# A transformer layer on one core: one GpSimd power moved ahead of a weight piece, the last high part given to VectorE, the final sums copied by token tile

## What is computed

```
h = patches @ W + b                        # 768 -> 192
q, k, v = split(h @ w_qkv.T)               # 12 heads of 64; q and k scaled by a norm over the heads
out = softmax(q k^T / scale) v             # 36 tokens of one image
h1 = layernorm(h + out @ w_out.T + b_out)                         # "LN1"
logits = h1 @ Wr + br                      # 8 experts, the two best are taken, softmax of the two
gate, up = split(min(h1 @ Wgu + bgu, 7))   # for each expert, 192 wide
act = (max(up, -7) + 1) * gate * sigmoid(1.702 * gate)
ffn = sum over the two experts of weight * (act @ Wd + bd)
h = layernorm(h1 + ffn)                                           # "LN2"
```

## Time and profile before

| | |
|---|---|
| runs | 142.15, 141.36, 141.29 us; median 141.36 |
| profiled execution | 141.29 us, span 139.4 us |
| granted TensorE clock, mean | 0.997 |
| TensorE busy | 131.2 us, 94% of the span |
| VectorE busy | 97.6 us, 70% |
| ScalarE busy | 77.6 us, 56% |
| GpSimd busy | 78.6 us, 56% |

### The profile page before, as it was taken

How to read it: one execution, slowest core, us unless ns; L and a number is a source line. 1 busy time by engine, 2 the same in 40 slices (tenths; PEclk the granted TensorE clock), 3 DMA queues, 4 the chain that set the end, 5 groups by cost and what they waited for, 6 DMA issues and landing times. The chain is left out here.

```text
span 139.4 us, 4023 instructions
## 1 busy us (share of the span) xinstructions
PE 131.2 (94%) x1585; PEld 122.3 (88%) x1586; DVE 97.6 (70%) x254; ACT 77.6 (56%) x150; POOL 78.6 (56%) x90
## 2 busy tenths in 40 slices
PE   6999899999999999996999999999998999999960
PEld 2779899999898889996989999999998989999940
DVE  0129589648959877646578687887798886688743
ACT  3057789989852557588468433144223455443671
POOL 7402158780478998999852863399552444244500
PEclk9999999999999999999999999999999999999998
DMA  4999964630122223322840000000000000000022
GB/s 133 302 375 405 413 218 121 219 113 0 28 56 54 69 68 93 127 81 78 296 167 0 0 0 7 0 0 0 0 5 0 0 0 0 7 0 2 0 65 62
DMA packets 5962, 12.42 MB, mean 89 GB/s; under 512 B 888, under 2 KB 2872, under 8 KB 5944
## 3 DMA queue, kind: packets, MB, share of 16 engines
q1 hardware_dynamic: 5944, 12.18, 25.8%
HBM read 9.96 MB, written 0.44 MB: 75 GB/s over the span
## 5 line engine op out<-in xcount | busy, mean ns | idle before, releaser
L476 POOL TENSOR_TENSOR reg_r<-reg_p,reg_r 128x324 fp32r<-128x324 f32 (+1 forms) x23 | 19.4, 843 | 21.9 <-ACT reg_r L708 21.9
L708 ACT ACTIVATE reg_r<-reg_p 128x324 fp32r<-128x324 f32 (+1 forms) x24 | 10.7, 444 | 29.0 <-DVE reg_p L1067 29.0
L408 POOL TENSOR_TENSOR reg_w<-stage,reg_w 128x768 fp32r<-128x768 f32 x12 | 22.6, 1887 | 5.2 <-ACT reg_w L540 5.2
L1271 PE MATMUL ps<-reg_r,reg_w 128*128 128x324 f32 (+1 forms) x48 | 14.8, 308 | 0.0
L1067 DVE SCALAR_TENSOR_TENSOR reg_p<-reg_q 128x324 f32<-128x324 f32 (+1 forms) x24 | 13.2, 552 | 2.2
L1044 DVE TENSOR_SCALAR reg_q<-ps,bup 128x324 f32<-128x324 f32 (+1 forms) x24 | 12.3, 511 | 3.1 <-PE ps L1275 3.0
L1272 PE MATMUL ps<-reg_r,reg_w 128*128 128x324 f32 (+1 forms) x48 | 14.2, 296 | 0.0
L1275 PE MATMUL ps<-reg_r,reg_w 128*128 128x324 f32 (+1 forms) x48 | 14.2, 295 | 0.0
L1273 PE MATMUL ps<-reg_r,reg_w 128*128 128x324 f32 (+1 forms) x48 | 14.2, 295 | 0.0
L1274 PE MATMUL ps<-reg_r,reg_w 128*128 128x324 f32 (+1 forms) x48 | 14.1, 295 | 0.0
L446 POOL TENSOR_TENSOR reg_q<-reg_q,rnorm 128x432 f32<-128x432 f32 x7 | 8.9, 1276 | 6.4 <-ACT rnorm L618 6.4
(11 more groups left out here) (196 smaller groups left out, 391.6 us busy)
## 6 DMA issues: line engine op xcount, KB each, us to landing
reg_x<-xw_in SPq DMA_DIRECT2D x5, 416.0 KB, 6.0
stage<-w_gu_a SPq DMA_DIRECT2D x4, 384.0 KB, 4.3
stage<-w_gu_b SPq DMA_DIRECT2D x4, 384.0 KB, 3.3
reg_r<-reg_x SPq DMA_DIRECT2D x24, 54.0 KB
stage<-w_qkv_a SPq DMA_DIRECT2D x3, 384.0 KB, 7.6
stage<-w_qkv_b SPq DMA_DIRECT2D x3, 384.0 KB, 8.0
stage<-w_down SPq DMA_DIRECT2D x3, 384.0 KB, 4.7
wout<-w_out SPq DMA_DIRECT2D x1, 576.0 KB, 9.6
```

The lines of the kernel that those rows point to most:

```text
L408: nc.gpsimd.tensor_tensor(dst[:, 1, :], raw, f(dst[:, 0, :]), ALU.subtract).then_inc(s_wlop, 1)
L476: nc.gpsimd.tensor_tensor(acts[:, n % NACT, 1, 0:w], act_f[:, n % 4, 0:w], f(acts[:, n % NACT, 0, 0:w]), ALU.subtract).then_inc(s_alo, 1)
L1271: mm(out_ap, w_a(0), x[:, 0, cols], start=True, stop=False)
```

## The change

It has four parts.

1. On GpSimd, piece 10's low part goes from behind probs(5), ahead of root(1), to behind root(1), ahead of probs(6). Piece 11 goes to the place of piece 12, 12 to that of 13, 13 to that of 14; piece 14 goes between act_lo(3) and act_lo(4), 15 between act_lo(4) and act_lo(5), 16's two instructions between act_lo(5) and act_lo(6) and behind act_lo(6).
2. On VectorE, z_tail(0) goes ahead of expert_act(13).
3. act_hi(23) goes from ScalarE to VectorE.
4. z_copy(1) and z_tail(1) become two instructions each, one for each token tile of 126; z_tiles(1) waits for each tile's own.

```
@@ gpsimd
                 if k in (3, 5, 6):
-                    w_lo({3: 7, 5: 9, 6: 11}[k])
+                    w_lo({3: 7, 5: 9, 6: 10}[k])
                 probs(k)
...
-                if k == 5:
-                    w_lo(10)
             root(2, TSIZES[2], s_ve, s_rstd)
-            w_lo(12)
+            w_lo(11)
             gap_exp(0)
             gap_exp(1)
             gap_exp(2)
             pool.wait_ge(s_w2, 6)
+            w_lo(12)
+            root(3, TSIZES[3], s_ve, s_rstd)
             w_lo(13)
-            root(3, TSIZES[3], s_ve, s_rstd)
-            w_lo(14)
             act_lo(0)
             act_lo(1)
             act_lo(2)
             root(4, TSIZES[4], s_ve, s_rstd)
             act_lo(3)
+            w_lo(14)
+            act_lo(4)
             w_lo(15)
-            act_lo(4)
+            act_lo(5)
             w_lo_full(16)
-            act_lo(5)
+            act_lo(6)
             w_lo_tail(16)
-            act_lo(6)
             gap_exp(3)
@@ shared
+        def z_parts(a):
+            return [slice(0, TS[0])] if a == 0 else [slice(ZS[1] * i, ZS[1] * i + ZS[1]) for i in range(ZN[1])]
@@ scalar
-                nc.scalar.activation(zT[:, 0, 0:TS[a]], ps[:, ACC, 0:TS[a]], ACT.Copy).then_inc(s_z, 1)
+                for cols in z_parts(a):
+                    nc.scalar.activation(zT[:, 0, cols], ps[:, ACC, cols], ACT.Copy).then_inc(s_z, 1)
...
-                act_hi(n if n >= NT + 4 else n - 1)
+                if n < 2 * NT - 1:
+                    act_hi(n if n >= NT + 4 else n - 1)
@@ vector
+            def act_hi(n):
+                dve.wait_ge(s_act, n + 1)
+                dve.wait_ge(s_ahi, n)
+                dve.wait_ge(s_dn, n - NACT + 1)
+                w = TS[n // NT]
+                nc.vector.tensor_copy(acts[:, n % NACT, 0, 0:w], act_f[:, n % 4, 0:w]).then_inc(s_ahi, 1)
...
-                nc.vector.tensor_copy(zT[:, 1, 0:TS[a]], ps[:, ACC + 1, 0:TS[a]]).then_inc(s_zd, 1)
+                for cols in z_parts(a):
+                    nc.vector.tensor_copy(zT[:, 1, cols], ps[:, ACC + 1, cols]).then_inc(s_zd, 1)
...
                     weigh(n - 1)
+                    if n == NT + 2:
+                        z_tail(0)
                     expert_act(n - 1)
...
-                if n == NT + 2:
-                    z_tail(0)
...
+            act_hi(2 * NT - 1)
             act_lo(2 * NT - 1)
@@ tensor, z_tiles
-                pe.wait_ge(s_z, a + 1)
-                pe.wait_ge(s_zd, a + 1)
...
+                    pe.wait_ge(s_z, 2 + i if a else 1)
                     nc.tensor.transpose(ps[0:n, b, o:o + DA], zT[:, 0, tok], ident[:, :])
+                    pe.wait_ge(s_zd, 2 + i if a else 1)
                     last = mm(ps[0:n, b, o + DA:o + D], zT[:, 1, tok], fold[:, 0:DB], start=True, stop=True)
```

## The result

The changed kernel takes 142.08 us (median of 22 runs) where the kernel before, on the same chip, takes 141.63 us: a ratio of 1.0033, 95% interval 1.002 to 1.0046. The forecast was 141.9 us from a profiled execution of 141.29, that is +0.61 us; measured is +0.47. The profiled execution has a span of 140.3 us, 0.9 more than before.

What follows compares the result with a forecast made beforehand. TensorE, busy in 94% of the span, was taken as the bound. Terms -1.0 + 1.8 + 0.24 - 0.33 - 0.1 = +0.61 us on the profiled 141.29 gave 141.9 us; range 140.0 to 142.7.

Steps and rivals of the forecast that it cites:

- Part 1, the power ahead: GpSimd's power ahead of piece 10: ln1(1) starts earlier and TensorE's wait at project(2) goes; -1.0 us, between 0 and -1.05.
- Part 1, the shift: Later pieces stand one place later on GpSimd, so gap_exp(3) delays router_weights(3) and TensorE's spreads; +1.8 us, +1.5 to +2.2.
- The count of the stretch: GpSimd from act_lo(3) to gap_exp(3): nine instructions without idle time instead of eight, putting gap_exp(3) 1.8 us later.
- Part 2, z_tail(0): VectorE, z_tail(0) ahead of expert_act(13): adds 0.40 us to the path, less 0.16 of stretch; +0.24 us, between 0 and +0.4.
- Part 3: Last down(23): act_hi(23) on VectorE removes TensorE's waiting in its last steps; -0.33 us, between -0.45 and -0.2.
- Part 4: Tail copies by token tile: TensorE's first transpose starts earlier; -0.1 us, between +0.05 and -0.15.
- Rival A: GpSimd or VectorE catches up, so the backlog does not reach TensorE; -1.2 us, 140.1 us; chance 0.17.
- Rival B: SBUF lock: expert_act(6) or expert_act(7) on VectorE waits on a GpSimd piece, 1.6 us on the path; 143.5 us; chance 0.09.
- Rival C: project(2) still starts near 65.3, held by another wait, so the 1.0 us gain is missing; 142.9 us; chance 0.07.
- VectorE's idle time "about 1.8 us longer": Expected sign in the profile after: VectorE's idle time before L1007 about 1.8 us longer, in one piece.

Runs made afterwards that it cites:

- The kernel in which the wait reappears at 70.58: Kernel before with piece 10 and root(1) exchanged on GpSimd and nothing else; measured ratio 1.0138 to the kernel before.
- the fastest one: Changed kernel with piece 16's two instructions moved to GpSimd's idle time ahead of act_lo(0) and act_lo(1), and z_tail(0) back behind expert_act(13); 139.83 us, ratio 0.9895.

## Why the prediction was right

- **Part 1, the power ahead.** -1.0 us forecast, -1.10 measured. The mechanism and its bounds held; GpSimd was idle before the third power as before (0.67 us).
- **Part 1, the shift.** +1.8 us forecast, +1.89 measured from the third power to router_weights(3), and TensorE's waits at the spreads in two pieces of 1.21 and 0.74 us, 1.95 in sum where 2.2 was forecast. The waits grew by 1.5 us only, but spread(10) itself comes 1.87 us later from the third power on: the matmul at the end of a wait takes 0.42 us instead of 0.31 and the start of the next is late with it. This term decides the sign. That it belongs to the order on GpSimd is shown by the kernel with that part alone (1.0087) and the kernel without it (0.9971); that it passes through gap_exp(3) is shown by the two kernels in which only that power moved, and by piece 16 out of the stretch.
- **The count of the stretch.** Nine instructions, as counted. The part of the stretch that falls away on the power (0.80 to 0.55 us) came, but the tail of piece 16 was stretched in its place (0.99 us where it took 0.74), so that the difference stayed at one piece.
- **Part 2, z_tail(0).** +0.24 forecast, +0.18 measured; undone, -0.17.
- **Part 3.** -0.33 forecast, -0.36 measured; undone, +0.35. The copy took 0.29 us, under both rows that I took for it, and 0.13 under a copy of its 252 columns from PSUM (0.42 us at 134.04 before). A column of such a copy costs some 0.8 ns (0.48 us at 324, 0.42 at 252), 252 columns 0.2 us, so the saving is about half of that or a little more (an estimate). **Part 4.** -0.1 and -0.11.
- **Rival A** (140.1) fell: nothing catches up between the power and weigh(9). The kernel that takes piece 16 out of the stretch without meeting the lock at the router steps gains what the backlog had cost, 1.84 us.
- **Rival B**, the lock, did not decide here but is real. expert_act(6) took 1.07 us instead of 0.50, which is 0.57 us, near the 0.65 that the rule of the Trainium skill (SBUF — State Buffer, Who interferes with whom) gave; the idle time before router_weights(3) hid it, as forecast, and that idle time is 1.14 us in place of 0.44 + 1.8 for the same reason: expert_act(7) lost another 0.55 us, so 1.1 of the more than 2 us at which B would have decided. Where the idle time was taken away, the lock came up as the next bound: it took 0.6 of 1.4 us when gap_exp(3) alone was moved, and most of the gain when piece 14 was.
- **Rival C** fell: project(2) starts at 64.60 with no wait.
- What the prediction put wrong: VectorE's idle time "about 1.8 us longer" (0.7 longer). That power's lateness and VectorE's own lateness overlap. It changed no sum, because the later of the two counts.

## What to carry to other kernels

Moving one instruction ahead of a long one pays only if the long one has a place to go: follow every later instruction that shifts with it to the next stretch of that queue without idle time, and ask who waits for its last member. Before a place in an engine's idle time is taken for free, look at what the other user of the same ports does then; here a weight piece in idle time cost 1.5 us beside a two-input VectorE instruction, and nothing where it ended 14 us ahead of the sensitive steps. And a tail item that trims 0.1 to 0.35 us is worth having, but is a twentieth to a fifth of the 1.9 us that the order at a busy place decides.

## What the runs showed of the hardware

**A VectorE instruction can wait for the end of a GpSimd one, whatever its own size.** A VectorE product with two SBUF inputs, 0.50 us alone, took 2.02 us when it began 0.17 us into a GpSimd piece of 1.84 us, and ended 0.35 us behind it; a cast of two columns, 0.15 us alone, took 0.58 beside act_lo and ended with it. The Trainium skill (SBUF — State Buffer, Who interferes with whom) names casts and tensor_scalar among those that can take the ports shared with GpSimd, where their operands meet its conditions. The traces agree, down to two columns.

**TensorE's clock near 71 us.** In the windows of the profiled execution of the kernel with GpSimd's new order alone, the columns are the window, busy time of PE, PEld, DVE, ACT and POOL, the granted clock, and the DMA's share and rate:

```profile
68.00:70.00 2.00, 1.91 (x52) 1.69 (x52) 1.41 (x8) 1.36 (x3) 2.00 (x2) 1.00 0.69 197
70.00:72.00 2.00, 2.00 (x35) 1.96 (x28) 1.22 (x8) 1.16 (x3) 0.62 (x2) 0.63 1.02 396
72.00:74.00 2.00, 2.00 (x9) 2.00 (x9) 1.78 (x15) 1.37 (x2) 0.55 (x1) 0.52 0.30 117
```

The clock falls from 2.4 to 1.2 GHz at about 70.5 us (granted clock 1.00 from 70.0 to 70.5, 0.52 from 70.5 to 71.0) and is back by 74, behind a stretch in which TensorE's work is logits of 16 columns, transposes and products of 36 columns. The same landmark as above, router_weights(3), is 101.97 - 62.46 = 39.51 us after the variance there and 37.95 in the changed kernel: 1.56 us. Of 93 executions of kernels with the wait at project(2) (75 of them of the kernel before, as timed beside the experiments), 7 had a mean granted clock under 0.986; of 92 executions of the experiments' kernels without it, 28. The changed kernel's own 22 executions, not among these, have 4. The kernel in which the wait reappears at 70.58 had 6 of 7, the fastest one 0 of 6. So a denser attention end goes with more such falls, but what in it brings them about was not tried, and stays open; it puts the measured ratio of some kernels above what their clean traces give.
